# A chain of four triangle-multiplication layers: x with partitions ordered (side, channel), centering as 64x64 blocks, constant rows kept in DRAM

## The reference

```
xn    = layernorm over the 64 channels of z, scaled and shifted
left  = (xn @ Wl + bl) * sigmoid(xn @ Wlg + blg)      # layers 0, 2: times a mask per token
right = (xn @ Wr + br) * sigmoid(xn @ Wrg + brg)
out   = for each of 64 channels a product of two 256x256 matrices:
        sum over k of left[i,k] * right[j,k]          # layers 0, 2
        sum over k of left[k,.] * right[k,.]          # layers 1, 3
out   = layernorm(out), gated by sigmoid(xn @ Wog + bog), projected by Wo (gate before Wo in
        layers 0 and 1, after it in layers 2 and 3)
```

## Time and profile before

| | us |
|---|---|
| median of 3 runs | 2225.65 (2222.49 to 2230.88) |
| the profiled execution | 2222.49 |
| its span | 2220.2 |
| granted TensorE clock, mean | 0.955 of full speed |
| TensorE busy | 1981.8 |
| VectorE busy | 1736.6 |
| ScalarE busy | 1691.7 |
| GpSimd busy | 625.2 |

### The profile page before, as it was taken

The page is one execution under the profiler, slowest core; times in us unless marked ns, Lnnn a source line. Parts: engine busy times, 40 slices in busy tenths (PEclk is TensorE's granted clock), DMA queues, the critical chain, the costliest instruction groups (busy, mean ns, idle before and its releaser), DMA issues. The chain is left out here.

```text
span 2220.2 us, 46598 instructions
## 1 busy us (share of the span) xinstructions
PE 1981.8 (89%) x13950; PEld 1408.4 (63%) x13956; DVE 1736.6 (78%) x2934; ACT 1691.7 (76%) x2730; POOL 625.2 (28%) x590
## 2 busy tenths in 40 slices
PE   5699889779899898989989899899998989899998
PEld 4433868645433887965633497887553359798665
DVE  6588899988688977878958896887775888687665
ACT  3488778779888866859978794776997888595676
POOL 0100647355300000016510190651872000000655
PEclk7799999999999999989999999999999999999999
DMA  9788956379788937358969992926997984663798
GB/s 396 286 253 258 285 139 181 104 259 356 287 253 265 323 106 251 128 209 344 415 226 284 267 233 90 286 80 226 393 404 218 285 302 157 220 221 124 289 347 302
DMA packets 437815, 557.91 MB, mean 251 GB/s; under 512 B 14896, under 2 KB 334384, under 8 KB 421296
## 3 DMA queue, kind: packets, MB, share of 16 engines
q1 hardware_dynamic: 434944, 538.38, 72.6%
q10 hardware_dynamic: 2736, 17.90, 1.9%
HBM read 380.05 MB, written 176.16 MB: 251 GB/s over the span
## 5 line engine op out<-in xcount | busy, mean ns | idle before, releaser
L772 PE MATMUL bank<-whigh,kept 128*128 128x128 f16 x4096 | 507.5, 227 | 59.1 <-DMA kept<-XH 19.0
L772 PEld LDWEIGHTS bank<-whigh,kept 128*128 128x128 f16 x4096 | 466.3, 125 | 68.2 <-issue 57.7
L772 PE MATMUL bank<-wlow,kept 128*128 128x128 f16 x4096 | 506.4, 227 | 1.3 <-issue 1.3
L772 PEld LDWEIGHTS bank<-wlow,kept 128*128 128x128 f16 x4096 | 467.0, 125 | 0.0
L1529 POOL TENSOR_TENSOR LR<-LR 128x512 f32<-128x512 f32 x128 | 187.0, 1480 | 525.0 <-DVE LR L1575 501.2
L794 ACT ACTIVATE sigs<-bank,small 128x256 f32<-128x256 f32 x512 | 236.6, 475 | 62.1 <-PE bank L772 55.6
L1520 POOL TENSOR_TENSOR LR<-LR,sum 128x2048 f32<-128x2048 f32 x30 | 136.6, 4552 | 513.0 <-DVE LR L1338 513.0
L635 PE MATMUL bank<-LR,cen 128*128 128x512 f32 x512 | 256.8, 627 | 21.2 <-DMA LR<-XT 9.2
L691 DVE SCALAR_TENSOR_TENSOR LR<-bank,small,LR 126x1024 f32<-126x1024 f32 x128 | 164.3, 1284 | 120.1 <-ACT LR L668 119.7
L794 ACT ACTIVATE squares<-bank,small 128x256 f32<-128x256 f32 x512 | 236.0, 475 | 13.6 <-PE bank L772 7.2
L643 PE MATMUL bank<-LR,kst 128*128 128x512 f32 x512 | 240.9, 593 | 5.2 <-ACT LR L664 5.2
(11 more groups left out here) (171 smaller groups left out, 3741.0 us busy)
## 6 DMA issues: line engine op xcount, KB each, us to landing
LR<-XT SPq DMA_DIRECT2D x128, 512.0 KB, 5.1
kept<-XH SPq DMA_DIRECT2D x128, 512.0 KB, 5.3
LR<-XT SPq DMA_DIRECT2D x64, 1024.0 KB, 9.6
kept<-XHA SPq DMA_DIRECT2D x128, 512.0 KB, 4.6
XT<-LR SPq DMA_DIRECT2D x48, 1024.0 KB, 8.7
LR<-XH SPq DMA_DIRECT2D x64, 512.0 KB, 6.5
LR<-XHA SPq DMA_DIRECT2D x64, 512.0 KB, 6.1
OS<-kept SPq DMA_DIRECT2D x12, 2048.0 KB, 7.5
```

What stands on the lines that cost most here:

```text
L772: last = pe.matmul(bank(g)[:, j * P:(j + 1) * P], tokens, w[:, half * P:(half + 1) * P], start=part == 0, stop=part == 1)
```

## The change

1. Partition 64s + c now holds channel c of side s. So `K_MEAN`, `K_GROUP` and `K_CENTER` become block-diagonal in halves of 64, the pairing copy and the copies to and from tokens change their inner strides, and `W_OUT` and its bias are laid out by halves.
2. `center(t)` issues four f32 matmuls of 64 rows by 64 columns of weights by 512 columns of x, one for each quarter of the array: side s reads partitions 64s to 64s+63, and the half `half` of the chunk's columns goes to output partitions 64 half to 64 half+63, in the PSUM bank of its side. A tile so holds on its partitions (half, channel), and in its columns (side, 512). `vary` stays two matmuls of 128x128.
3. `scale` and `halve` work on all 128 partitions; high and low are stored by half (`store_xh`: four DMAs per chunk in all layers). The left-out channel is now channel 0, dropped when reading: `XH` and `XHA` have 65 rows, and loads take rows 1 to 64.
4. Row 64 holds the constants. Two small VectorE memsets and six DMAs in the very first block write them once; the memsets of `norm` on GpSimd go.
5. The loads of the projection in layers 0 and 2 are four DMAs of 256 KB instead of two of 512 KB.

Most of the diff (the layouts in `constants` and `pack` last, cut):

```diff
@@ -115,8 +115,8 @@
...
         XT = nc.dram_tensor("XT", [NT, 8, P, COLS], F32).ap()
-        XH = nc.dram_tensor("XH", [NT, C, 2, 2, 8, 8, 256], F16).ap()
-        XHA = nc.dram_tensor("XHA", [C, 2, 2, NT, N // 2, P], F16).ap()
+        XH = nc.dram_tensor("XH", [NT, C + 1, 2, 2, 2, 4, 8, 256], F16).ap()
+        XHA = nc.dram_tensor("XHA", [C + 1, 2, 2, NT, N // 2, P], F16).ap()
...
@@ -257,23 +257,15 @@
...
-        def xh_rows(n, s, k_is_b):
-
-            if k_is_b:
-                return XH[bass.ds(n // 8, 1), :, :, s, :, bass.ds(n % 8, 1), :] \
-                    .rearrange("o c w v g f -> (o c w) v (g f)")
-            return XHA[:, :, s, :, bass.ds(8 * n, 8), :].rearrange("c w t j a -> (c w) t (j a)")
-
...
-            if k_is_b:
-                for s in range(2):
-                    sp.dma_start(XH[bass.ds(n // 8, 1), :, part, s, :, bass.ds(n % 8, 1), :]
-                                 .rearrange("o c v g f -> (o c) v (g f)"), xh_cols(buf[s::2, :], k_is_b)) \
-                        .then_inc(stored_.s, 16)
-            else:
-                sp.dma_start(XHA[:, part, :, :, bass.ds(8 * n, 8), :].rearrange("c s t j a -> c s t (j a)"),
-                             xh_cols(buf, k_is_b)).then_inc(stored_.s, 16)
+            for t in range(2):
+                if k_is_b:
+                    to = XH[bass.ds(n // 8, 1), 0:C, part, t, :, :, bass.ds(n % 8, 1), :] \
+                        .rearrange("o c s v g f -> (o c) (s v) (g f)")
+                else:
+                    to = XHA[0:C, part, :, t, bass.ds(8 * n, 8), :].rearrange("c s j a -> c s (j a)")
+                sp.dma_start(to, xh_cols(buf[C * t:C * t + C, :], k_is_b)).then_inc(stored_.s, 16)
...
@@ -308,7 +300,14 @@
...
             for s in range(2):
-                sp.dma_start(xh_cols(xh_b[h][s], k_is_b), xh_rows(n, s, k_is_b)).then_inc(landed[h].s, 16)
+                if not k_is_b:
+                    sp.dma_start(xh_cols(xh_b[h][s], k_is_b),
+                                 XHA[1:C + 1, :, s, :, bass.ds(8 * n, 8), :].rearrange("c w t j a -> (c w) t (j a)")) \
+                        .then_inc(landed[h].s, 16)
+                for t in range(2 if k_is_b else 0):
+                    sp.dma_start(xh_b[h][s][:, 1024 * t:1024 * t + 1024].rearrange("p (v f) -> p v f", v=4),
+                                 XH[bass.ds(n // 8, 1), 1:C + 1, :, t, s, :, bass.ds(n % 8, 1), :]
+                                 .rearrange("o c w v g f -> (o c w) v (g f)")).then_inc(landed[h].s, 16)
...
@@ -418,6 +419,13 @@
...
                     sp.sem_inc(s.s, CREDIT)
+                sp.wait_ge(rows_set.s, rows_set.n + 2)
+                for part, row in enumerate(last_rows):
+                    for t in range(NT):
+                        sp.dma_start(XH[t, C, part, :, :, :, :, :].rearrange("e s v g f -> (e s v g) f"), row[:, 0:256]) \
+                            .then_inc(rows_set.s, 16)
+                    sp.dma_start(XHA[C, part, :, :, :, :].rearrange("s t j a -> j (s t) a"),
+                                 row.rearrange("p (x a) -> p x a", a=P)).then_inc(rows_set.s, 16)
...
@@ -426,6 +434,8 @@
...
             def _(dve):
+                dve.memset(last_rows[0], X_SCALE).then_inc(rows_set.s, 1)
+                dve.memset(last_rows[1], 0.0).then_inc(rows_set.s, 1)
...
@@ -492,7 +502,7 @@
...
                         dve.wait_ge(enter_turned.s, enter_turned.n + 4 * n - 4)
-                        dve.tensor_copy(e_x[n % 2].rearrange("p (v c s) -> p s v c", s=2, c=C),
+                        dve.tensor_copy(e_x[n % 2].rearrange("p (v s c) -> p s v c", s=2, c=C),
...
@@ -593,8 +603,7 @@
...
             cb, k_is_b = small[:, 7:8], layer["k_is_b"]
-            per, tiles = 64 if k_is_b else 32, 2 * NCH
-            kept = P - 2
+            per, tiles = 64, 2 * NCH
...
@@ -627,13 +637,15 @@
...
                     pe.wait_ge(normed.s, normed.n + t - 2)
-                    for u in range(2):
-                        at = 2 * (t % 2) + u
-                        cols = xa[h][:, at * BANK:(at + 1) * BANK] if k_is_b else \
-                            xa[h].rearrange("p (g j r) -> p j g r", g=16, j=8)[
-                                :, 4 * (at % 2):4 * (at % 2) + 4, 8 * (at // 2):8 * (at // 2) + 8, :]
-                        last = pe.matmul(banks[t % 3][:, u * BANK:(u + 1) * BANK], cen[:, :], cols,
-                                         start=True, stop=True)
+                    u = t % 2
+                    for half in range(2):
+                        for s in range(2):
+                            rows = slice(C * s, C * s + C)
+                            cols = xa[h][rows, (2 * half + u) * BANK:(2 * half + u + 1) * BANK] if k_is_b else \
+                                xa[h][rows, :].rearrange("p (g j r) -> p j g r", g=16, j=8)[
+                                    :, 4 * u:4 * u + 4, 8 * half:8 * half + 8, :]
+                            last = pe.matmul(banks[t % 3][C * half:C * half + C, s * BANK:(s + 1) * BANK],
+                                             cen[rows, rows], cols, start=True, stop=True)
...
@@ -675,34 +687,29 @@
...
-            @block.gpsimd
-            def _(pool):
-                for h in range(4):
-                    pool.wait_ge(stored[h].s, stored[h].n)
-                for h in range(2):
-                    pool.memset(high[h][96:P, :], X_SCALE).then_inc(rows_set.s, 1)
-                    pool.memset(low[h][96:P, :], 0.0).then_inc(rows_set.s, 1)
...
                     dve.wait_ge(lows_ready.s, lows_ready.n + t - 3)
-                    dve.scalar_tensor_tensor(yc[t % 4][0:kept, :], banks[t % 3][0:kept, :], cb[0:kept, :],
-                                             rs[t % 4][0:kept, :], ALU.add, ALU.mult).then_inc(normed.s, 1)
+                    dve.scalar_tensor_tensor(yc[t % 4], banks[t % 3][:, :], cb, rs[t % 4], ALU.add, ALU.mult).then_inc(normed.s, 1)
...
-                    h, cols = t // 2 % 2, slice((t % 2) * GW, (t % 2 + 1) * GW)
+                    h = t // 2 % 2
+                    y, to, rest = (v.rearrange("p (s f) -> p s f", s=2) for v in (yc[t % 4], high[h], low[h]))
+                    to, rest = (v[:, :, t % 2 * BANK:(t % 2 + 1) * BANK] for v in (to, rest))
...
                         dve.wait_ge(stored[h].s, stored[h].n + per * (t // 4))
-                    dve.tensor_copy(high[h][0:kept, cols], yc[t % 4][0:kept, :]).then_inc(highs_ready.s, 1)
+                    dve.tensor_copy(to, y).then_inc(highs_ready.s, 1)
                     dve.wait_ge(highs_ready.s, highs_ready.n + t + 1)
-                    dve.tensor_tensor(low[h][0:kept, cols], yc[t % 4][0:kept, :], high[h][0:kept, cols],
-                                      ALU.subtract).then_inc(lows_ready.s, 1)
-
-                dve.wait_ge(rows_set.s, rows_set.n + 4)
+                    dve.tensor_tensor(rest, y, to, ALU.subtract).then_inc(lows_ready.s, 1)
+
+                dve.wait_ge(rows_set.s, rows_set.n)
+                for h in range(4):
+                    dve.wait_ge(stored[h].s, stored[h].n)
...
@@ -899,10 +907,10 @@
...
                 if layer["k_is_b"]:
-                    sp.dma_start(buf, XH[ut, :, part, :, vb, :, :].rearrange("c s g f -> c s (g f)")) \
+                    sp.dma_start(buf, XH[ut, 1:C + 1, part, vb // 4, :, vb % 4, :, :].rearrange("c s g f -> c s (g f)")) \
...
                 else:
-                    sp.dma_start(buf, XHA[:, part, :, ut, 16 * vb:16 * vb + 16, :].rearrange("c s j a -> c s (j a)")) \
+                    sp.dma_start(buf, XHA[1:C + 1, part, :, ut, 16 * vb:16 * vb + 16, :].rearrange("c s j a -> c s (j a)")) \
...
@@ -1485,7 +1493,7 @@
...
                     act.activation(nat[c % 2].rearrange("p (s v c) -> p v s c", s=2, c=C)[:, 4 * q:4 * q + 4, :, :],
-                                   bank(t % 2).rearrange("p (j c s) -> p j s c", j=4, s=2),
+                                   bank(t % 2).rearrange("p (j s c) -> p j s c", j=4, s=2),
...
@@ -1617,18 +1625,19 @@
...
     k = np.zeros((P, K_END), np.float32)
-    same_half = np.arange(P)[:, None] % 2 == np.arange(P)[None, :] % 2
-    channel = np.arange(P) // 2
-    k[:, K_CENTER:K_CENTER + P] = np.eye(P) - same_half / C
-    k[:, K_CENTER_OUT:K_CENTER_OUT + P] = np.eye(P) - (np.arange(P)[:, None] // C == np.arange(P)[None, :] // C) / C
-    k[:, K_MEAN:K_MEAN + P] = same_half / C
-    k[:, K_GROUP:K_GROUP + P] = (channel[:, None] // 2 == channel[None, :] // 2) / 4
+    same_side = np.arange(P)[:, None] // C == np.arange(P)[None, :] // C
+    pair_of = np.arange(P) % C // 2
+    row = np.arange(P) // 2
+    k[:, K_CENTER:K_CENTER + P] = np.eye(P) - same_side / C
+    k[:, K_CENTER_OUT:K_CENTER_OUT + P] = np.eye(P) - same_side / C
+    k[:, K_MEAN:K_MEAN + P] = same_side / C
+    k[:, K_GROUP:K_GROUP + P] = (pair_of[:, None] == pair_of[None, :]) / 4
     k[:, K_IDENT:K_IDENT + P] = np.eye(P)
-    drop = (np.arange(C)[:, None] == channel[None, :]).astype(np.float32)
-    drop[C - 1, :] = -1
```

(23 more changed lines are left out.)

## The result

The changed kernel took **2258.7 us** in the median of 4 runs (2255.0 to 2260.5), the kernel before 2224.2 in the same session: ratio **1.0147, 95% interval 1.0122 to 1.0173**. It is slower by 34.5 us. I had said 2299, 73 us slower: the direction held, the size was less than half, and what makes it slower is not what I had named.

The account below looks back on a forecast made before the run. The norm's loop of waits was taken to bound at 3.69 us a tile, TensorE close behind at 3.44. 2222.5 + 72 (TensorE) + 1.5 (constant rows) = 2296, as median 2299; own range 2270 to 2335, with rivals from 2195.

Parts of the forecast that it names:

- The centering matmuls: Norm: four 64x64 matmuls, eight passes, overlap only between neighbours in program order; 2.13 us a tile, 0.42 more than now.
- Five slots: Centering order: quarters A to D, first (1) and second (2) passes, 0.43 us a slot, B1 queued behind A2; 2.13 us.
- The change of array shape: Norm: switching between centering's 64x64 and vary's 128x128 costs 0.20 us, seen in the weights' fold; 0.40 us a tile.
- TensorE's sum: Norm: centering 2.13, vary 1.72 and shape changes 0.40 make 4.25 us a tile for 3.69; +72 us in all.
- Rival 1: Norm: all quarters run at once, centering 0.86 us, 3.46 us a tile; 2207 us in the median, chance 0.22.
- that loop: Norm's chain of waits: scale, center, vary, Ln, Exp, scale, two tiles each time; 3.69 us a tile before, 4.10 forecast.
- ScalarE's floor of 3.3: Norm: ScalarE's own work stops any gain at 3.3 us a tile; 2177 us if it alone bounds.
- Stores and loads: Norm, SP's queue: layers 1 and 3 loads leave 1.5 us later, 11.9 us needed, 12.7 available; covered, 0 us.
- Rival 2: Norm: quarters overlap, but XT's load behind the stores takes over, 3.65 to 3.7 us a tile; 2220 to 2232, chance 0.13.
- Constant rows: First block: SP's hold hidden because VectorE waits for x until 8.26 us, bytes written show; +1.5 us, ends 0 and 6.
- Loads of the projection: Layers 0 and 2: four loads for two per chunk, 2 x 0.58 us more issue, just hidden; 0, at most 1 us each.
- The lower end of the forecast's range: Overlap as taken and shape steps at 0 us a tile: +48 us, 2270 in all.

Follow-up runs that it names:

- experiment 1: The changed kernel with every centering matmul of the norm issued twice; 2266.8 us, ratio 1.0201.
- experiment 8: The changed kernel with stores one chunk later, constant-row stores behind the loads of x, and vary as four 64x64 matmuls; 2200.9 us, ratio 0.9902.
- experiment 2: The changed kernel with each chunk's stores issued one step later on SP, behind the load of XT; 2208.7 us, ratio 0.9939.
- experiment 5: The kernel before with new stores: layers 0 and 2 from 64 neighbouring partitions, layers 1 and 3 four for two over all partitions; 2238.8 us, ratio 1.0071.
- experiment 6: The kernel before with the changed kernel's stores in all four layers, each from 64 neighbouring partitions, matmuls as before; 2250.2 us, ratio 1.0142.
- experiment 4: The kernel before with each chunk's stores one chunk later on SP's queue; 2222.0 us, ratio 0.9990.

## Why the prediction was wrong, step by step

- **The centering matmuls, the step that failed.** "A1, then A2 with B1, B2 with C1, C2 with D1, D2. Five slots, 2.13 us". Measured 1.09 us, of which 0.86 is streaming: the first passes of all quarters start within 0.02 us, and four more matmuls cost 0.86 (experiment 1). I had carried the order seen among full-array passes over to quarters and taken B's first pass to stand behind A's second. The records show four first passes and then four second passes, so that queue is not there. This step alone was +0.42 us a tile for -0.86, 164 us over the kernel if TensorE had bounded in both cases.

  The Trainium skill's rule that speaks for the overlap, tiles working in parallel (TensorEngine Tiling (Array Packing), "Key Properties"), agrees with this trace. The one on strict program order (TensorE: Matmul & The Clock Gate, Part 3) speaks of whole matmuls. These rows do not contradict it; my use of it for single passes they do.
- **The change of array shape: right.** 0.20 us predicted from the fold. Experiment 1 has 0.16 us into vary and 0.19 out of it beyond the streaming (1.88 and 1.91 for 1.72), experiment 8 has 0.11 into vary. The Trainium skill (TensorEngine Tiling (Array Packing), "Key Properties") says that a change of tiling mode drains TensorE, with which these times agree.
- **TensorE's sum: wrong by the first step.** Predicted 4.25 us a tile; experiment 1 gives 3.79 - 0.86 = 2.93. The kernel of experiment 2, which doesn't wait for XT, runs at 3.42 to 3.52. Rival 1 had 3.46 for that loop, and ScalarE's floor of 3.3 stands.
- **Stores and loads, "covered: 0": wrong for the kernel as it is.** I had kept the landing as it was because bytes and packets stay. But a store out of 64 neighbouring partitions lands in 3.9 us for 3.0, and in 3.6 for 2.5 (experiments 5 and 6), and the load behind it leaves and lands later. From the end of the scale, where my sum starts, to the centering it is now 13.9 us (144.33 to 158.21), while three tiles of a loop of 3.46 leave 10.4. The sum was short even for the kernel before: 12.7 us in the same place (154.10 to 166.77), not 10.9, since the second load landed 6.1 us after its issue and not 4.6. The term that I had at 0 carries the loss in the norm: +26 us by the stores alone in experiment 6, +27 in the whole change. The sentence that followed, "if TensorE became faster instead, this cover would be gone", is what happened. The Trainium skill has the rule that I passed over (SBUF — State Buffer, "Door 1: The DMA port swizzle"): a transfer whose partitions are all in 0 to 63, or all in 64 to 127, reaches only half of SBUF's 16 ports. The landing times agree with it; that the ports are the reason, no run here shows by itself.
- **Rival 2: the right place, the wrong price.** It named the load behind the stores on SP's queue, and experiment 2 shows that place. It said 2220 to 2232. Missing were the later landing, and the clock. After the four waits in the norm of layer 0 TensorE's next centering and vary take 8.8 us more in all than undisturbed ones, after the single such wait in layer 2 2.7 us more; layer 0 runs at 4.01 us a tile, layer 2 at 3.80. That speaks for a part of the loss. Against it stands experiment 6: there the matmuls wait 1.8 us at most in that layer, the clock stays at 0.99, and the norm loses as much. How much of the 27 us is the clock, no run separates.
- **Constant rows: +1.5, measured 4.9,** within the bound of 0 to 6. What was wrong is that VectorE waits for x until 8.26 anyway. SP starts the six issues only at 7.28, so that even 3 us of them would have shown, and ends them at 13.2, some 6 us in all and not 3. The bytes themselves cost nothing that shows. That the memsets on GpSimd gave nothing, no run tests by itself.
- **Loads of the projection:** the median issue of one is 0.37 us, so four take some 0.35 us more than two at 0.58, not 1.16. Waits for their data grew, but mostly in experiment 6 too, with the old loads; this is part of the 6 us left open.
- **The lower end of the forecast's range:** wrongly added. With no shape step its terms give 3.85 us for TensorE and 3.90 for the loop, +27 us and some 2254, not +48 and 2270. That 2258.7 lies above 2254 says nothing for the mechanism, for the five slots are in that sum as well.

The two errors in the norm have opposite signs. TensorE got 0.2 us a tile faster where I had said 0.56 slower, and the stores took away that gain and 0.22 more. Slower came out by a mechanism that I had priced at nothing: the direction was right by luck, for the wrong reason.

## What to carry to other kernels

In this kernel four f32 matmuls of 64x64 on the four quarters took the time of one, plus 0.1 to 0.2 us at each change to another array shape: price both. When partitions are laid out anew, look at which partitions each DMA then touches: here 256 KB out of 64 neighbouring ones landed in 3.9 us, out of every second one in 3.0, and the load behind them on the queue paid too. And when the engine that bounds gets faster, the order on the DMA queue has to be set again. One step of lag between stores and loads was worth 50 us after the change and nothing before it, so try the pair, not the one edit.

## What the runs showed of the chip that I had not expected

- f32 matmuls on different quarters: first passes start within 0.02 us of each other, and the second passes 0.48 us later.
- The same eight passes take 1.09 us, or up to 1.99 after TensorE has waited 2.8 to 4.0 us, at a granted clock of 0.50; after some waits of 2.8 us they still take 1.09. The mean clock of layer 0's norm falls from 0.98 to 0.90 by four such waits.
- Time from issue to landing of a 256 KB store: 3.0 us from every second partition, 3.9 from 64 neighbouring ones; in the form of layers 1 and 3, with longer packets, 2.5 from all partitions, 3.6 from 64 neighbouring ones. The old stores behind a load instead of before it: 4.2 and 4.5 instead of 3.0 (experiment 4).
- Six small stores (64 and 128 KB) took SP 5.9 us: the first three 0.42 to 0.44 us each, the next two 1.98 together, the last 2.13. The median issue of a 256 KB load in the changed kernel's projection is 0.37 us.
